# Quantising the last layer's weights in 12 chunks of 512 columns from the eighth expert pair on, instead of 24 of 256 from the second

## What is computed

```python
def _mx_dequant(t):
    blocks = t.reshape(rows, feat // 32, 32)
    max_abs = jnp.max(jnp.abs(blocks), axis=-1)
    scales = jnp.maximum(max_abs / 448.0, 1e-30)
    q = (blocks / scales[..., None]).astype(jnp.float8_e4m3fn).astype(jnp.float32)
    return (q * scales[..., None]).reshape(rows, feat)
gate = _mx_dequant(x2d) @ _mx_dequant(gate_w).T      # up_w and down_w likewise
```

## Time and profile before

| | us |
|---|---|
| median of 3 runs | 470.87 |
| lowest and highest | 468.99, 473.08 |
| the profiled execution | 472.56 |
| its span, first to last instruction | 469.6 |

### The profile page before, as it was taken

The page is one execution under the profiler, slowest core; times in us unless marked ns, Lnnn a source line. Parts: engine busy times, 40 slices in busy tenths (PEclk is TensorE's granted clock), DMA queues, the critical chain, the costliest instruction groups (busy, mean ns, idle before and its releaser), DMA issues.

```text
span 469.6 us, 8464 instructions
## 1 busy us (share of the span) xinstructions
PE 389.5 (83%) x2840; PEld 281.2 (60%) x2840; DVE 334.9 (71%) x781; ACT 177.8 (38%) x419; POOL 240.2 (51%) x355
## 2 busy tenths in 40 slices
PE   2658898896498999999598977789868999898865
PEld 2547777685375566787385755667654555455544
DVE  2778877568857355988475288688676999999990
ACT  2355875225035455543244524153452122112220
POOL 4465556533278676776212778563121554544541
PEclk9898999899679899999999999799999999999996
DMA  8897877535939987789843453331100000000000
GB/s 255 270 270 180 182 162 183 154 112 121 171 101 219 265 226 197 216 178 193 160 143 107 135 163 109 113 103 61 43 3 0 0 13 11 12 3 10 11 11 22
DMA packets 71509, 57.40 MB, mean 122 GB/s; under 512 B 38054, under 2 KB 63788, under 8 KB 71468
## 3 DMA queue, kind: packets, MB, share of 16 engines
q1 hardware_dynamic: 66304, 43.76, 34.1%
q0 software_dynamic: 4608, 12.59, 12.8%
q10 hardware_dynamic: 556, 0.53, 0.4%
HBM read 42.18 MB, written 14.68 MB: 121 GB/s over the span
## 4 chain that ended last, share of the span: by engine, by line
PE 32%; issue 17%; POOL 17%; DVE 16%; DMA 8%; SPq 5%; ACT 4%; ACTq 0%; POOLq 0%; DVEq 0%
PE psum L1291 6%; DMA ys_dram<-stage 4%; SPq L436 4%; POOL arena_dn L687 4%; POOL arena_up L625 3%; POOL mx_w L690 3%; PE psum L1481 3%; DMA shared<-h_dram,tok_u 3%; PE psum L1508 2%; PE psum L1301 2%; PE psum L1306 2%; PE psum L1490 2%; PE psum L1580 2%; PE psum L1350 2%; PE psum L1511 2%
## 5 line engine op out<-in xcount | busy, mean ns | idle before, releaser
L601 POOL DMA_INDIRECT shared<-h_dram,tok_u x64 | 63.0, 984 | 38.1 <-PE psum L1291 15.0
L1611 PE MATMUL psum<-arena_dn 128*128 128x512 f32 x128 | 57.1, 598 | 3.2 <-ACT arena_dn L840 3.2
L687 POOL TENSOR_TENSOR arena_dn<-arena_dn 128x512 f32<-128x512 f32 x16 | 20.3, 1270 | 45.6 <-DVE arena_dn L1122 45.6
L1611 PEld LDWEIGHTS psum<-arena_dn 128*128 128x128 f32 x128 | 23.7, 190 | 31.3 <-issue 26.3
L1291 PE MATMUL psum<-ident,arena_up 128*128 128x128 f32 x144 | 24.8, 287 | 14.2 <-DVE arena_up L1182 2.9
L625 POOL DMA_INDIRECT arena_up<-ys_dram,slot_u x32 | 31.2, 975 | 10.6 <-issue 10.6
L1153 DVE TENSOR_TENSOR h1T<-psum,h1T 128x128 f32<-128x128 f32 x32 | 9.3, 291 | 37.9 <-ACT h1T L788 37.2
L1706 PE MATMUL psum<-arena_dn,mx_w 128*128 128x256 f32 x128 | 31.5, 403 | 0.4 <-ACT mx_w L850 0.3
L1291 PEld LDWEIGHTS psum<-ident,arena_up 128*128 128x128 f32 x144 | 16.6, 143 | 23.2 <-DVE arena_up L1246 5.1
L801 ACT COPY stage<-psum 128x512 f32<-128x512 f32 x32 | 18.7, 585 | 28.9 <-DMA ys_dram<-stage 16.2
L1291 PE MATMUL psum<-ident,arena_dn 128*128 128x128 f32 (+1 forms) x97 | 16.8, 284 | 15.3 <-DMA arena_dn<-in_L_xattn_v_img_b_dram 7.8
(11 more groups left out here) (232 smaller groups left out, 1003.4 us busy)
## 6 DMA issues: line engine op xcount, KB each, us to landing
ys_dram<-stage SPq DMA_DIRECT2D x32, 256.0 KB
arena_up<-in_L_ffn_wg_dram SPq DMA_DIRECT2D x8, 512.0 KB, 5.4
arena_up<-in_L_ffn_wu_dram SPq DMA_DIRECT2D x8, 512.0 KB, 7.1
arena_dn<-in_L_ffn_wd_dram SPq DMA_DIRECT2D x64, 64.0 KB
arena_dn<-in_L_ffn_wd_dram SPq DMA_DIRECT2D x3, 1024.0 KB, 7.8
va_dram<-stage SPq DMA_DIRECT2D x8, 256.0 KB, 2.7
kT_dram<-stage SPq DMA_DIRECT2D x8, 256.0 KB, 2.4
arena_up<-kT_dram SPq DMA_DIRECT2D x8, 256.0 KB, 2.6
```

The source lines that it names most:

```text
L601: pool.indirect_dma_start(out=xg[n % 4][:, b, :], out_offset=None, in_=h1_dram[:, :], in_offset=bass.IndirectOffsetOnAxis(ap=tok_u[:, 2 * ...
L687: pool.tensor_tensor(haF[h], haF[h], heF[h], ALU.subtract).then_inc(sem("hint"), 1)
L1611: ins = pe.matmul(bank[2 * part + h][:, :], xTF[n % 2][:, c, :], mx_gu[:, c, lo:lo + HW], start=(c == 0), stop=(c == C - 1))
```

## The change

`WC` goes from 256 to 512 and with it the number of chunks from 24 to 12. Every operation of a chunk is twice as wide. `weight_halves` now gives none for steps up to 7, and one half a step from step 8 to step 31. The chunk that waits for down_w is number 8 in place of number 16, both of which begin at column 4096. TensorE's group n waits for one chunk more in place of two. The scratch row `we` had a place of its own in SBUF; it now lies behind the four gather buffers in the tile `shared`, in a part that held the shared experts' down weights. The rows of scales (`wam`, `wac`, `war`) become 16 wide in place of 8.

```diff
-WC = 256
+WC = 512
 NWC = 6144 // WC
@@ def weight_halves(n)
-    return min(max(min(n, NPS - 1), 0) + 2 * max(n - NPS + 1, 0), 2 * NWC)
+    return min(max(n - 7, 0), 2 * NWC)
@@ build_program
         take = carver(shared)
         xg = [take(2, D) for _ in range(4)]
         xgT = [xgT1.rearrange("p (b c j n) -> p b c j n", b=2, c=C, j=Q)]
+        we = take(WC)
@@
-        we = sb("we", [P, WC])
         wam = sb("wam", [P, WC // QB])
@@ weight_half(h)
-                    if n == 16:
+                    if n == 8:
                         dve.wait_ge(sem("mx_in2"), 16 * 4)
@@ mx_turns()
-                    pe.wait_ge(sem("w_deq"), 2 * n + 2)
+                    pe.wait_ge(sem("w_deq"), n + 1)
```

## The result

| | us |
|---|---|
| changed kernel, median of 20 runs | 474.49 (469.37 to 479.54) |
| kernel before, median of 20 runs beside it | 471.56 (465.85 to 477.69) |
| ratio, with its 95% interval | 1.007 [1.0043, 1.0096] |
| profiled execution of the changed kernel | 474.61, span 472.9 |

The account below looks back on a forecast made before the run. The prediction took TensorE, then DMA late in the pairs, to bound the stretch. Every term was 0, so the sum of 0 on the 470.87 us median gave 470.9 us, range 465.0 to 475.0.

Parts of the forecast that it names:

- The pairs are bound by TensorE and then by DMA: Expert pairs: TensorE busy throughout 160 to 208 us, then idle 6.2 us to 236 for DMA; less VectorE work gains 0.
- VectorE's work: Weight quantising: a 512-column chunk costs 3.99 us, twelve 47.9; 23.3 us less VectorE work, off the path.
- Pairs 8 to 15: Where work is added: VectorE's mean 2.39 us a pair fits under the 2.963 us period, 0.57 spare; cost 0.
- rival 2: Pairs 8 to 15: VectorE, held by POOL's rescale and gathers, becomes the pace; 4.3 us more, 475.2 us; chance 0.11.
- POOL: Pairs 8 to 15: the rescale grows by 0.425 us and fits with 0.26 left in two pairs; cost 0.
- rival 3: Pairs 8 to 15: POOL becomes the pace; 1.2 us more, 472.1 us; chance 0.03.
- The end of the pairs: After the last pair: one half follows instead of three, weights ready some 2 us earlier, covered by a store; gain 0.
- Rival 1: Gathers after 208 us: slow because VectorE holds POOL's port; relief would remove 6.2 us, giving 464.7 us; chance 0.17.

Follow-up runs that it names:

- place alone: Kernel before with only the scratch row moved behind the gather buffers, still 256 wide: 484.08 us, ratio 1.0007 [0.9964, 1.0051].

## Why the prediction held

- **The time.** I predicted 470.9 us, which was the median of before and a sum of 0; the kernel before came out at 471.56 beside the changed kernel's 474.49. The sum of 0 is borne out by the mechanism below. Of the 3.6 us above my number 0.7 are the kernel before itself; for the other 2.9 I have no cause. The range took them in because it was made wide for rivals that did not come true, and that is luck more than insight.
- **The pairs are bound by TensorE and then by DMA.** Right, and shown from both sides: without any quantising the time is 1.0017 of before, and with the DMA wait taken away TensorE fills the stretch although VectorE is busier than before, 24.2 of 28 us in place of 18.9.
- **VectorE's work.** I had a chunk at 3.99 us and a saving of 23.3 us; it measured 4.16 and 21.3. The reciprocal was 0.253 in place of 0.203, and the small scale averaged 0.273 where I took the undisturbed 0.175. The term was off by 2 us and lay off the path.
- **Pairs 8 to 15.** I had 2.39 us of VectorE a pair under a period of 2.963, with 0.57 to spare. The period stayed at 2.962, and the idle time ahead of the multiply was 0.91 and 0.37 us in turn, 0.64 in the mean. Over the whole loop the multiply waited for the Silu in 30 of 32 pairs (22 before). A load of 4.5 us a pair set the pace, as rival 2 has it; one of 3.17 against a pace of 3.13 cost nothing that the waits show.
- **POOL.** The rescale took 1.056 us for the 1.047 taken, but the spare time was mis-sized. I counted all of the 0.69 us ahead of a gather as free, while 0.30 of it stands ahead of a gather anyway. That leaves 0.69 - 0.30 - 0.425, nothing to spare. In the trace the rescales are 5.97 and 6.00 us apart where two pairs take 5.93: POOL did run over, by about 0.06 us in each two pairs. The four buffers took that up, and TensorE was busy throughout, so rival 3 cost nothing that shows.
- **The end of the pairs.** I had the weights ready 2 us ahead and worth nothing. The last rescale ended at 255.59 us, 1.96 us ahead of the end of the last output copy (257.55), and the first gather of the next stage again came 2.8 us behind the first weight turn. It began at 260.41 us in place of the 257.7 that I had named, because the pairs had begun 3.3 us later.
- **Rival 1.** Its doubling from 0.22 to 0.44 us a packet is real, and without it TensorE's 6.2 us of idle time are gone; its cause was wrong. It survives with VectorE idle and goes with the addresses. By the Trainium skill, "SBUF — State Buffer", section "Who interferes with whom", VectorE's fast modes block POOL's descriptor writing. A gather instruction took 0.947 us in the median before, 0.949 in the changed kernel and 0.946 without any quantising, so that no run here shows a gain from fewer such instructions. The changed kernel had about half the time in them (13.5 us for 24.4), and 0.25 and 0.44 us a packet.
- **The 0.7% of the first measurement.** They were not reproduced (0.9968 and 0.9995). In the one profile of that measurement the extra time lay ahead of the pairs. What that stretch does differently from one execution to the next I did not settle. That the first measurement caught a small real effect that the two others don't show isn't excluded.

## What to carry to other kernels

Before moving hidden work, leave it out altogether once: that bounds what a new schedule of it can be expected to gain, here by 0.25%. Work out the period of the loop and what each engine has to do in it; the work is free up to that, and most of what goes beyond is paid. Take the period from the same chip, and don't count as spare the gap that stands ahead of every instruction anyway. When a transfer's packets slow down in one stretch, look at the addresses and at the padding of the data before looking at the engines beside it: slots that carry nothing should still gather from different rows.

## What the runs showed of the hardware that I had not expected

- With every empty slot reading row 0, a packet of the gathers (2.7 KB in the mean, 1.46 MB in 543) took 0.44 us of an engine's time late in the pairs; with the rows spread, 0.16. How many of those packets are of empty slots the traces don't say. The stores in the other queue were slow with them: one took 13 us to land, in the earlier trace rows.
- The same kernel before took 472 us on one chip and 485 on two others. With place alone, a pair of the fixed experts took 3.13 us on a slower one, in place of 2.963, with VectorE idle over 1 us in each. The waits of the profiles on the slower chips also have a releaser that the other profiles don't show. The longest of it in the changed kernel's second profile:

```profile
ACT h1T L788 <- remote: 5.9, 2, 5.1
```

  What it stands for, no run here shows. It is one more reason to compare only runs of one chip.
